# The routed tiles of two experts: transposes, norms and low halves in another order, and one weight copy given to GpSimd

## The reference

```python
x = x + gnn(_layernorm(x), ...)                      # graph attention, 4 heads of 64
x = x + ffn(_layernorm(x)[None], ...)[0]             # routed experts
# ffn, for each expert i:
h = gelu(x @ W1[i] + b1[i])                          # 1024 -> 64
h = gelu(h @ W2[i] + b2[i])                          # 64 -> 64
y = h @ W3[i] + b3[i]                                # 64 -> 1024
outputs += y * w                                     # w = mean over the top 2 of (index == i)
```

## Time and profile before

| | us |
|---|---|
| median of 3 runs | 2071.55 (2068.31 to 2073.85) |
| profiled execution | 2072.07 |
| its span | 2070.2 |
| busy PE / DVE / ACT / POOL | 1664.8 / 1294.7 / 773.1 / 782.8 |

### The profile page before, as it was taken

How to read it: one execution, slowest core, us unless ns; L and a number is a source line. 1 busy time by engine, 2 the same in 40 slices (tenths; PEclk the granted TensorE clock), 3 DMA queues, 4 the chain that set the end, 5 groups by cost and what they waited for, 6 DMA issues and landing times.

```text
span 2070.2 us, 27922 instructions
## 1 busy us (share of the span) xinstructions
PE 1664.8 (80%) x8625; PEld 1335.5 (65%) x8625; DVE 1294.7 (63%) x2446; ACT 773.1 (37%) x1342; POOL 782.8 (38%) x758
## 2 busy tenths in 40 slices
PE   4999999999586553988889883878888778888886
PEld 3788888888442232767667662666666666666665
DVE  4555555555165753767567673777777767776775
ACT  3444444444133440010000002555555545555554
POOL 1211111122188201456645533344444444444453
PEclk9999999999888895888888886999999999999999
DMA  9344444441544236878778774566566566566421
GB/s 244 84 129 123 124 120 120 119 119 40 144 118 116 91 110 144 199 208 226 204 200 229 203 210 119 154 175 191 173 178 175 170 169 177 162 174 183 115 52 34
DMA packets 131732, 311.77 MB, mean 151 GB/s; under 512 B 69071, under 2 KB 80597, under 8 KB 120017
## 3 DMA queue, kind: packets, MB, share of 16 engines
q1 hardware_dynamic: 62175, 181.56, 33.9%
q0 software_dynamic: 66208, 108.34, 18.2%
q10 hardware_dynamic: 3234, 20.48, 3.2%
HBM read 188.85 MB, written 138.85 MB: 158 GB/s over the span
## 4 chain that ended last, share of the span: by engine, by line
PE 45%; DMA 18%; DVE 13%; issue 7%; POOL 6%; ACT 5%; SPq 4%; DVEq 0%; POOLq 0%; ACTq 0%
DMA cx<-in_x 12%; PE psum L1527 12%; PE psum L1529 10%; PE psum L1528 10%; DVE xt_lo L1444 5%; DVE xb L1463 4%; PE psum L1552 4%; PE psum L1545 3%; PE psum L1808 2%; DMA agg<-node_table,from_idx 2%; POOL xls L613 2%; ACT xt_hi L851 2%; PE psum L1839 2%; POOL td L617 2%; ACT gl L865 1%
## 5 line engine op out<-in xcount | busy, mean ns | idle before, releaser
L1527 PE MATMUL psum<-xt_hi,st_w 128*128 128x256 f32 x528 | 179.5, 340 | 139.4 <-DVE xt_lo L1444 136.4
L693 POOL DMA_INDIRECT out<-xb,idx_in x132 | 185.2, 1403 | 154.1 <-DVE xb L1463 123.0
L851 ACT ACTIVATE xt_hi<-psum 128x512 fp32r<-128x512 f32 x264 | 150.7, 596 | 226.0 <-PE psum L1808 210.6
L1444 DVE TENSOR_TENSOR xt_lo<-psum,xt_hi 128x512 fp32r<-128x512 f32 x264 | 175.5, 683 | 87.7 <-ACT xt_hi L851 76.7
L1527 PEld LDWEIGHTS psum<-xt_hi,st_w 128*128 128x128 f32 x528 | 103.7, 196 | 182.7 <-DVE xt_lo L1444 177.3
L1284 DVE TENSOR_TENSOR cx<-cx,psum 125x512 f32<-125x512 f32 x160 | 108.4, 678 | 131.0 <-DMA cx<-in_x 104.1
L824 ACT ACTIVATE aggt_hi<-psum 128x500 fp32r<-128x500 f32 x40 | 22.6, 586 | 435.9 <-PE psum L1724 435.9
L955 DVE TENSOR_TENSOR axt_lo<-psum,axt_hi 128x500 fp32r<-128x500 f32 x160 | 108.5, 678 | 120.8 <-ACT axt_hi L725 120.8
L845 ACT ACTIVATE xn<-xb 128x1024 f32<-128x1024 f32 x132 | 156.3, 1231 | 60.1 <-DMA xb<-rows_x,idx_in 60.1
L684 POOL DMA_INDIRECT xb<-rows_x,idx_in x132 | 142.4, 1079 | 86.3 <-POOL xb L680 54.0
L1808 PE MATMUL psum<-ident,xn 128*128 128x128 f32 x1056 | 154.6, 281 | 24.9 <-ACT xn L845 24.8
(11 more groups left out here) (280 smaller groups left out, 4405.7 us busy)
## 6 DMA issues: line engine op xcount, KB each, us to landing
rows_x<-cx SPq DMA_DIRECT2D x20, 1806.0 KB
cx<-in_x SPq DMA_DIRECT2D x20, 1792.0 KB
ax<-in_x SPq DMA_DIRECT2D x19, 1792.0 KB
st_half<-experts SPq DMA_DIRECT2D x66, 512.0 KB
node_table<-trow ACTq DMA_DIRECT2D x19, 896.0 KB
node_table<-xld SPq DMA_DIRECT2D x10, 500.0 KB
st_half<-experts SPq DMA_DIRECT2D x66, 64.0 KB
rows_x<-cx SPq DMA_DIRECT2D x20, 209.6 KB
```

Of the source, the lines that this page charges most:

```text
L693: pool.indirect_dma_start(out=out[:, :], out_offset=bass.IndirectOffsetOnAxis(ap=idx_in[:, t % NI, s:s + 1], axis=0), in_=xb[:, b, s, 0:D] ...
L851: act.activation(xt_hi[:, 2 * q:2 * q + 2, :].rearrange("p k n -> p (k n)"), T_R[q % 2], ACT.Copy).then_inc(r_hi, 1)
L1444: dve.tensor_tensor(xt_lo[:, 2 * q:2 * q + 2, :].rearrange("p k n -> p (k n)"), T_R[q % 2], xt_hi[:, 2 * q:2 * q + 2, :].rearrange("p k n ...
L1527: pe.matmul(out_ap, left[0], right[0], start=start, stop=False, skip_group_check=True)
```

## The change

It touches the tile stage on four engines, and no arithmetic.

- PE: the first two transposes of tile t + 1 go from behind the last down products to between `down(t - 1, 1)` and `hidden2(t)`; the other two transposes of a tile go each ahead of a piece of `hidden1`.
- ACT: `norm_r` of tile t + 1 is split. Its first half goes ahead of `gelu_1(t)`, its second behind it, followed by `high_r(t + 1, 0)` and `(t + 1, 1)`, which stood behind `gelu_2(t)`. The register load of the pair goes behind the first norm.
- DVE: both `stage_w1` copies go ahead of `low_1`; `lower_w2` and the first two `low_r` of tile t + 1 go ahead of `low_2(t)`; `lower_w3` is gone.
- POOL: `lower_w3(t)`, a register load from the tile table and a copy of 64 lanes by 2048 numbers, stands between `take_rows(t + 2)` and `put_rows(t - 1)`.
- ACT also waits once for the split expert weights, and POOL once for the table.

```diff
--- before.py
+++ after.py
@@ -696,14 +696,23 @@
                         in_=xb[:, b, s, 0:D], in_offset=None, bounds_check=N - 1, oob_is_err=False
                     ).then_inc(rows_out[b], 16)
 
+            def lower_w3(t):
+                e = pool.value_load(tile_tab[0:1, 1, t:t + 1], min_val=0, max_val=SLOTS - 1)
+                wait(pool, r_y, 4 * (t - 1))
+                pool.tensor_copy(st_half[0:EH, t % 2, 0:2 * D],
+                                 experts[0:EH, bass.ds(e, 1), 0:2 * D].rearrange("p a b -> p (a b)")).then_inc(r_w3, 1)
+
             for b in range(3):
                 pool.wait_ge(x1_put[b], 32 * ((NG - b + 2) // 3))
+            pool.wait_ge(r_tab, 1)
             take_rows(0)
+            lower_w3(0)
             take_rows(1)
             for t in range(NT):
                 if t + 2 < NT:
                     take_rows(t + 2)
                 if t >= 1:
+                    lower_w3(t)
                     put_rows(t - 1)
             put_rows(NT - 1)
 
@@ -837,13 +846,13 @@
                     upper_half(g - S0)
 
 
-            def norm_r(t):
+            def norm_r(t, s):
                 b = t % NX
-                act.wait_ge(rows_in[b], 32 * (t // NX + 1))
-                wait(act, r_tp, 4 * t)
-                for s in range(NS):
-                    act.activation(xn[s][:, :], xb[:, b, s, 0:D], ACT.Identity, bias=xb[:, b, s, D + 1:D + 2],
-                                   scale=xb[:, b, s, D:D + 1]).then_inc(r_xn, 1)
+                if s == 0:
+                    act.wait_ge(rows_in[b], 32 * (t // NX + 1))
+                    wait(act, r_tp, 4 * t)
+                act.activation(xn[s][:, :], xb[:, b, s, 0:D], ACT.Identity, bias=xb[:, b, s, D + 1:D + 2],
+                               scale=xb[:, b, s, D:D + 1]).then_inc(r_xn, 1)
 
             def high_r(t, q):
                 act.wait_ge(r_tp, 4 * t + q + 1)
@@ -883,22 +892,26 @@
                 return act.value_load(tile_tab[0:1, 3, t:t + 1], min_val=0, max_val=PAIRS - 1)
 
             act.wait_ge(r_tab, 1)
+            act.wait_ge(half_lo, 2 * SLOTS)
             act.wait_ge(x1_put[0], 32 * ((NG + 2) // 3))
-            norm_r(0)
+            for s in range(NS):
+                norm_r(0, s)
             high_r(0, 0)
             high_r(0, 1)
             for t in range(NT):
-                pair = pair_of(t)
+                more = t + 1 < NT
                 high_r(t, 2)
                 high_r(t, 3)
+                if more:
+                    norm_r(t + 1, 0)
+                pair = pair_of(t)
                 gelu_1(t, pair)
-                if t + 1 < NT:
-                    norm_r(t + 1)
+                if more:
+                    norm_r(t + 1, 1)
+                    high_r(t + 1, 0)
+                    high_r(t + 1, 1)
                 gelu_2(t, pair)
                 choose(t, pair)
-                if t + 1 < NT:
-                    high_r(t + 1, 0)
-                    high_r(t + 1, 1)
 
 
         @block.vector
@@ -1479,11 +1492,6 @@
                 dve.tensor_copy(st_half[0:EH, t % 2, 2 * D:BUNDLE],
                                 experts[0:EH, bass.ds(e, 1), 2 * D:BUNDLE].rearrange("p a b -> p (a b)")).then_inc(r_w2, 1)
 
-            def lower_w3(t, e):
-                wait(dve, r_y, 4 * (t - 1))
-                dve.tensor_copy(st_half[0:EH, t % 2, 0:2 * D],
-                                experts[0:EH, bass.ds(e, 1), 0:2 * D].rearrange("p a b -> p (a b)")).then_inc(r_w3, 1)
-
             dve.wait_ge(r_tab, 1)
             e = first_of(0)
             stage_w1(0, 0, e)
@@ -1491,7 +1499,6 @@
             dve.wait_ge(half_lo, 2 * SLOTS)
             dve.wait_ge(x1_put[0], 32 * ((NG + 2) // 3))
             lower_w2(0, e)
-            lower_w3(0, e)
             low_r(0, 0)
             low_r(0, 1)
             for t in range(NT):
@@ -1501,21 +1508,19 @@
                 if more:
                     e = first_of(t + 1)
                     stage_w1(t + 1, 0, e)
+                    stage_w1(t + 1, 1, second_of(t + 1))
                 low_1(t)
-                if more:
-                    stage_w1(t + 1, 1, second_of(t + 1))
                 if t >= 1:
                     result(t - 1, 0)
                     result(t - 1, 1)
+                if more:
+                    lower_w2(t + 1, e)
+                    low_r(t + 1, 0)
+                    low_r(t + 1, 1)
                 low_2(t)
                 if t >= 1:
                     result(t - 1, 2)
                     result(t - 1, 3)
-                if more:
-                    lower_w2(t + 1, e)
-                    low_r(t + 1, 0)
-                    low_r(t + 1, 1)
-                    lower_w3(t + 1, e)
             for u in range(4):
                 result(NT - 1, u)
 
@@ -1845,22 +1850,22 @@
             turn_r(0, 0)
             turn_r(0, 1)
             for t in range(NT):
+                turn_r(t, 2)
                 hidden1(t, 0)
-                turn_r(t, 2)
+                turn_r(t, 3)
                 hidden1(t, 1)
-                turn_r(t, 3)
                 hidden1(t, 2)
                 hidden1(t, 3)
                 if t >= 1:
                     down(t - 1, 0)
                     down(t - 1, 1)
+                if t + 1 < NT:
+                    turn_r(t + 1, 0)
+                    turn_r(t + 1, 1)
                 hidden2(t)
                 if t >= 1:
                     down(t - 1, 2)
                     down(t - 1, 3)
-                if t + 1 < NT:
-                    turn_r(t + 1, 0)
-                    turn_r(t + 1, 1)
             for u in range(4):
                 down(NT - 1, u)
 
```

## The result

The changed kernel takes 2125.36 us (median of 4 runs, 2120.24 to 2127.12), the one before 2071.12 on the same chip (2068.31 to 2073.85): a ratio of 1.0233, 95% interval 1.0208 to 1.0258. It is slower, where 2048 was forecast, and lies 15 us outside the range. The profiled execution has a span of 2123.2 us against 2070.2.

The account below looks back on a forecast made before the run. POOL's serial list was taken to bound filled tiles, 11.75 us against 11.89 (-7), and PE's loop the empty ones, 10.05 against 11.60 (-17): -24 on 2072.07 gives 2048, own range 2030 to 2066, with rivals 1998 to 2110.

Parts of the forecast that it names:

- PE's part: PE's loop per tile: the wait for the first low half goes, so 11.60 us becomes 10.05; empty tiles gain 17 us.
- new wait of 0.5: PE, after the downs: the second norm on ACT ends at 6.6 us against the downs' end at 6.15.
- POOL's copy: On POOL between gathers and puts: copying 2048 numbers a lane takes 2.0 us, with bounds 1.85 and 4.7.
- the load's 0.4: On POOL: the register load added with the copy, estimated at 0.4 us a tile.
- the gap's 0.31: On POOL: the gap between two transfers with no load in it, entered in POOL's loop as 0.31 us.
- the second loop: Rows, norm, results, puts, landing and next gather into the same buffer half span two tiles: 11.5 us a tile, confirming the size.
- The term of 7.7: From the first norm, now ahead of `gelu_1`, to that iteration's last result on DVE: about 7.7 us.
- The sum for POOL: POOL's serial loop in filled tiles: 8.3 us plus landing 3.2 plus collisions 0.25 gives 11.75, against 11.89 before.
- Rival 2: Between gathers and puts, POOL's copy makes POOL slower than before: 12.5 us a filled tile, 2091 us; chance 0.26.
- Rival 4: Nothing comes of it: some new wait, such as late rows ahead of the first norm, keeps 2072 us; chance 0.05.
- Rival 1 and 3: Puts' queue absorbs the copy, 2003 us, chance 0.23; PE bounds everywhere and POOL does not matter, 1957 us, chance 0.03.
- POOL's wait for DVE's results gone in filled tiles: Sign expected in the profile after, on POOL ahead of the puts; before, this wait was 92.7 us in 37 tiles.

Follow-up runs that it names:

- the filler's kernel: Kernel after plus 36 products that nothing reads, on PE ahead of the next tile's transposes in every second iteration: ratio 1.0227 to the kernel before.
- with whole tiles: Kernel after with its three orders undone and `lower_w3` early on DVE, POOL's list not split by halves: 1.0058 to the kernel before, 2087.02 us.
- with the memset moved: Kernel with orders undone and copy early on DVE, plus POOL's memset moved from ahead of the gathers to behind the puts: 0.9962, 2068.44 us.
- with halves: Orders undone, copy early on DVE, memset behind puts, plus POOL's gathers and puts interleaved by half tiles, each with its own semaphore: 0.9548, 1984.31 us.

## Why the prediction was wrong

**PE's part was right.** 10.05 us were forecast for a tile without rows to move. With the copy off POOL it is 10.03, and eight transposes in such a tile wait 0.48 for ACT's norm, the forecast new wait of 0.5. In the kernel after it is 11.1, since the lock reaches `low_2`, whose stall was costed at nothing under PE's slack.

**POOL's copy was right in length.** 2.0 forecast, 1905 ns measured:

```profile
L702 POOL CAST st_half<-experts 64x2048 fp32r x66 | 125.7, 1905 | 0.2
...
L693 POOL DMA_INDIRECT out<-xb,idx_in x132 | 139.6, 1058 | 159.6 <-DVE xb L1476 129.9 <-issue 29.8
```

Of the load's 0.4 and the gap's 0.31, 0.17 are left. The put fell from 1306 ns to 1058, as forecast. POOL's serial part is 2.34 + 1.90 + 0.17 + 2.31 + 0.97 = 7.7, under the 8.3 of the sum.

**The step that failed is the second loop**, "rows, norm, results, puts, landing and the next gather". It was computed as 11.5 and used as a confirmation of the size, without a rival of its own. Measured in one pair of tiles against its terms (forecast in brackets): rows 7.80 (8.75), norm to put 10.88 (7.7), puts 2.31 (2.3), landing 3.69, then 0.15 for the memset and 0.87 to the gather (3.2 + 0.97). That is 25.7 against 22.9. The term of 7.7 is the one that fails, by 3.2; on average it measured 10.4, with rows at 9.0, and the mean over all filled tiles, 13.12, lies 0.3 above this pair's 12.9. By parts: to the transposes 3.32 (3.23); the transposes to the start of `hidden2` 1.59 (1.04); `hidden2` and the two last downs, 1655.83 to 1660.27, 4.44 (2.26, at full clock from the earlier trace rows); the last result and the way to the put 1.53 (1.1, without the 0.84 between the two). So 2.7 of the 3.2 are PE at half clock, which the loop itself brings about by making PE stand. But the clock is not the whole error: with it back, in the filler's kernel, norm to put is still 9.9, since DVE's `low_2` beside POOL's copy, priced at nothing, then comes last. The loop that was held equal to POOL's list was the bound.

**The sum for POOL** (11.75 with a landing of 3.2) was then not what bounds: POOL waits 1.53 us a tile for DVE and 3.78 for landings, the former in every second tile, 3.19 on average in the even ones. The forecast had it that POOL's slack was gone.

**The rivals.** Rival 2, POOL's copy makes it slower, has the right sign and was given 0.26 with 2091. Its middle of 12.5 lies under both of the loops that it adds up, 13.0 and 12.75; with these it would have said 2118 and 2105. Its mechanism is real, 130 us by itself in the kernel before, though there by DVE's stalls and not by POOL's list, where POOL stands 3.2 us ahead of a tile's puts. In the kernel after it is not the cause of the slower filled tiles, since the version without the copy on POOL is as slow. That the sign came out right is luck. Rival 4 names the place, "the rows' late arrival ahead of the first norm, which now holds `gelu_1` too", at 0.05, and priced it at no change. Priced by the loop that it closes it would have been the slower case. Rival 1 and 3 did not occur. "POOL's wait for DVE's results gone in filled tiles" was wrong: 79.5 us against 92.7.

Some later expectations were too good in the same way. Undoing the orders was to give 2000 to 2060 and gave 2091, one edit at a time was to open the loop and did not, and the memset was to give 26 and 48 us and gave next to none in the filled tiles. The first and the last took the wait for landing as a constant to subtract from; it grew when the puts went out earlier, 5.86 against 4.12.

## What to carry to other kernels

When work of the next tile is moved ahead of work of the last one, go down each in-order list and write which results now stand behind which input. If the input's buffer is freed by those results, a loop runs from input to result to transfer to buffer: add up its path before and after. Here it grew from 5.8 to 10.4 us between norm and put, and that cost more than the wait removed. Undoing one of several such orders shows little, because the others keep the path long. Price the path with what each engine has beside it: here PE after standing, at half clock, and DVE beside POOL's copy. And a faster compute loop pays only when the list that issues the transfers doesn't wait for its own landings: here one and the same order of work ran 0.6% slower than before with whole tiles, 0.4% faster with the memset moved, and 4.5% faster with halves.

## What was not expected of the hardware

- A GpSimd copy of 64 by 2048 numbers takes 1.90 us and holds up DVE's subtraction of two operands in SBUF (0.43 us alone, 1.93 and 2.67 in the rows above) and, with a gather's issue beside it too, its copy of 128 by 1024 (0.695 on average before, 3.02 here, in the kernel before with POOL's copy):

```profile
2124.08 3.02 DVE L1482 CAST st_w<-w_tab 128x1024 fp32r x1 [0.33 <-issue]
```

  DVE's subtraction with an operand in PSUM kept its 0.69 us (688 ns on average in the kernel after).
- PE stood 4.67 us and was then at 0.50 of its clock from 1654 to 1660 us. What it ran there took almost twice as long (1.94 against 1.04), and keeping it busy brought the clock back to 0.99 and the filled tiles from 13.12 to 12.67, without bringing the time back.
